# One long kernel of eight layers: other written orders of the pieces on five engines, and other places of the idle matmuls

## The reference, cut to what matters

```
x = x + L0_attn_a(ln(x))   # a recurrent state of 8x8 per head, one step per token (16 heads)
x = x + L0_ffn(ln(x))      # 8 experts, the best 2 by softmax, and a shared one (swiglu)
x = x + L0_attn_b(ln(x))   # best 15 of all earlier tokens, gathered; small MLP; a sampled palette
x = x + L0_ffn(ln(x))
x = x + L1_attn_a(ln(x))   # linear attention, running sums
x = x + L1_ffn(ln(x))      # 8 experts in bf16, the best 2 by sigmoid, and a shared one (relu squared)
x = x + L1_attn_b(ln(x))   # decaying state per head
x = x + L1_ffn(ln(x))
```

```
delta  = clip(v_t - k_t.S, -1, 1);  S = S + clip(0.9 * k_t delta, -1, 1);  o = clip(S.q_t, -1, 1)
```

## Time and profile before

| | us |
|---|---|
| timed runs: lowest, median, highest of 3 | 1463.68, 1468.32, 1477.88 |
| the profiled execution, first to last instruction | 1461.1 |
| PE busy, of which fill matmuls (585) | 1240.4, of which 178.1 |
| DVE busy | 1039.1 |
| POOL busy | 974.7 |
| ACT busy | 790.6 |
| first and last step of the scan on DVE | 44.3, 1196.8 |

### The profile page before, as it was taken

The page is one execution under the profiler, slowest core; times in us unless marked ns, Lnnn a source line. Parts: engine busy times, 40 slices in busy tenths (PEclk is TensorE's granted clock), DMA queues, the critical chain, the costliest instruction groups (busy, mean ns, idle before and its releaser), DMA issues.

```text
span 1461.1 us, 47169 instructions
## 1 busy us (share of the span) xinstructions
PE 1240.4 (85%) x18481; PEld 807.8 (55%) x18481; DVE 1039.1 (71%) x4444; ACT 790.6 (54%) x2119; POOL 974.7 (67%) x1398
## 2 busy tenths in 40 slices
PE   3787787888898988888899989988998989898886
PEld 1333444555556565655656565655656565656654
DVE  2778877888777877787687777978788775463532
ACT  1232243556466565658465556657474647566754
POOL 2553767786967677786776687877757567765541
PEclk9777687989999999999889999999899989999999
DMA  6000101001000000000000000100001010101000
GB/s 172 1 2 5 29 12 29 22 17 28 9 19 19 16 18 10 26 12 21 12 26 11 12 22 10 28 8 22 14 4 33 8 35 11 31 15 30 4 2 7
DMA packets 27208, 29.54 MB, mean 20 GB/s; under 512 B 12097, under 2 KB 22114, under 8 KB 26978
## 3 DMA queue, kind: packets, MB, share of 16 engines
q0 software_dynamic: 8304, 16.73, 4.4%
q1 hardware_dynamic: 18674, 9.71, 2.4%
HBM read 25.10 MB, written 2.29 MB: 19 GB/s over the span
## 4 chain that ended last, share of the span: by engine, by line
PE 36%; POOL 24%; DVE 20%; issue 9%; ACT 8%; SPq 1%; DMA 1%; POOLq 0%; DVEq 0%; ACTq 0%
POOL sb L1784 5%; POOL sb L1649 4%; DVE ps L964 4%; POOL sb L1646 3%; PE ps L665 3%; PE ps L717 3%; DVE ps L956 2%; PE ps L523 2%; PE ps L563 2%; PE ps L778 2%; PE ps L577 2%; POOL sb L1850 2%; PE ps L587 1%; PE ps L864 1%; PE ps L604 1%
## 5 line engine op out<-in xcount | busy, mean ns | idle before, releaser
L964 DVE TENSOR_TENSOR_SCAN ps<-ps,sb 128x47 f32<-128x47 f32 (+3 forms) x1024 | 271.0, 265 | 45.6 <-ACT sb L1373 1.5
L1784 POOL DMA_INDIRECT sb<-table,sb x240 | 244.7, 1020 | 86.7 <-issue 48.9
L956 DVE TENSOR_TENSOR ps<-sb,ps 128x24 f32<-128x24 f32 (+3 forms) x1024 | 193.2, 189 | 15.9
L523 PE MATMUL ps<-sb 128*128 128x512 bf16 x585 | 178.1, 415 | 7.7 <-ACT sb L1581 3.1
L1646 POOL TENSOR_TENSOR sb<-sb 128x1 f32<-128x1 f32 x128 | 74.4, 581 | 136.2 <-DVE sb L899 135.3
L1649 POOL TENSOR_SCALAR sb<-sb 128x128 f32<-128x128 f32 x128 | 103.8, 811 | 22.8 <-POOL sb L1646 22.0
L1297 ACT ACTIVATE sb<-ps 128x128 f32<-128x128 f32 x128 | 35.2, 277 | 136.4 <-PE ps L535 135.5
L577 PE MATMUL ps<-sb 32*32 32x32 f32 x2032 | 70.2, 209 | 43.6 <-DVE sb L936 42.6
L577 PEld LDWEIGHTS ps<-sb 32*32 32x32 f32 x2032 | 41.4, 108 | 114.0 <-DVE sb L936 72.2
L587 PEld LDWEIGHTS ps<-sb 32*32 32x32 f32 x2032 | 42.1, 108 | 100.2 <-issue 50.0
L587 PE MATMUL ps<-sb 32*32 32x12 f32 x2032 | 64.9, 189 | 28.9 <-DVE sb L972 21.5
(11 more groups left out here) (307 smaller groups left out, 3541.1 us busy)
## 6 DMA issues: line engine op xcount, KB each, us to landing
sb<-table,sb POOLq DMA_INDIRECT x240
sb<-in_cs SPq DMA_DIRECT2D x16, 128.0 KB
table<-sb SPq DMA_DIRECT2D x17, 64.0 KB, 1.5
sb<-in_x SPq DMA_DIRECT2D x4, 256.0 KB, 8.6
sb<-dscr SPq DMA_DIRECT2D x64, 2.0 KB
out<-sb SPq DMA_DIRECT2D x16, 64.0 KB
sb<-in_mdn POOLq DMA_DIRECT2D x1, 512.0 KB, 10.3
sb<-in_wex SPq DMA_DIRECT2D x1, 512.0 KB, 6.8
```

The source lines that it names most:

```text
L523: e.matmul(b[:, 0:512], identb[:, :], mup[:, 0:512], start=True, stop=True)
L956: e.tensor_tensor(at(psP, p + ROW - 3 - 2 * m, [ROW, 3], [2, m], [1, 2]), AC[:, row(n, k), :, HIST - 2 * m:HIST].rearrange("p r (a b) -> p ...
L964: e.tensor_tensor_scan(at(psD, 16 + k + COMB * skip, [COMB, 3 * ROW - skip]), at(psP, p + skip, [1, 3 * ROW - skip]), Q[:, i % 32, skip:3 ...
L1784: e.indirect_dma_start(GA[:, k, :], None, table[0:128 * i + 128, :] if i else table0, bass.IndirectOffsetOnAxis(u[:, k:k + 1], 0)).then_in ...
```

## The change

The strings of `ORDER` for all five engines and the digits of `FILL` are others. No instruction's form, tile or wait is changed. Each engine keeps the same number of pieces of each letter, so every real instruction of before is there again. Most pieces stand a few places earlier or later than before. On VectorE the letters of the scan shift by at most 7 places in 3856. The number of ScalarE's table loads stays at 60.

`FILL` now sums to 652 in place of 585. By the 20 rows of 112 digits: the first row has 79 in place of 98; the next fourteen (pieces 112 to 1679, which run from 139 to 1076 us in the trace of before) have 380 in place of 256; the last five have 193 in place of 231. Of these matmuls, 140 in place of 101 stand at pieces of the scan (letter s).

The diff replaces 104 lines of letters and digits; here are the first of TensorE's order, all of SyncE's, and the first and tenth of FILL:

```diff
@@ -107,116 +107,116 @@
 ORDER = {
     "PE":
...
-        "sfffsggffssggssfssgsfsssssgsssfssssssgsssssgsfsssgosoosossssffgssoossosasasasgsssaassasasasasgsssppfsssspsso"
...
+        "ffsfggffsgssgssfssgfsgssfsssssssssssssgsssgsfssssgosoosossossffssgossosasssaasgssaasassasasassgspspfssssssps"
...
     "SP":
-        "ppppmpppmpppmppmpppmppppmppppmppmppppmpmpppppmpmpppmppepemeppppmpeepemeeeeeeeeee",
+        "pppmpppmpppmpppmppppmepepppmeppmppemppppmepppempppepmepmppepmppeppmpppepmpmeeeee",
 }
 FILL = (
-    "0919090620400000025030020200100001010000101000001000500001020200007000090100000102000000000000002020000200020000"
...
-    "0001200000000000300000000010000000000000000010000000000000000040000000000000000000000000000000000000000020000000"
...
+    "3109100100002010005500000000000300000000200140003000600000002000030050060000000001002000000003000120000400000003"
...
+    "0001010000000000020000400000000002000200000000100000000100000000200003000000100000020010000000000003000000000000"
...
```

More of the change, by code:

```diff
@@ L115 @@
[L115 to L124, removed]
@@ new lines @@
+    "ACT":
+        "ffffffffffgffgsfffgfsfffffggffffsgsffggfffssffgooofooooffsfgffoaaaaaagsgppffpsffpfsppppogoooogooosaaaaaappps"
+        "ffffgsfmfmppmsmpgoppppfffffofooooomgmpmomfmmppsaafffaaammfpasgpgsmposoooooofffffmmmmpppgoppaagaaasmmpgfmmapp"
+        "mfmffpbbsfmbmbbbfppmlssollgooooollfffffommlgmmlppppopccsccccccccacccgcafmmfsaaadpmmaddddmffgfmmmfbgsbbbpogbf"
+        "fffpffopbppooooosmlllgmomlmllpmppaglppapaacapsgcccccsmcccccmpcccpmemefeeeseeeemmaeeeedddeddmmfffgbsbofmbbboo"
+        "ppobooommfmmfffpfplslolpppplllaagpplafaammgfmmacccccmcccmccccccmssmfeffeeepeeeeeedeebeeddfddmbbobbppgboooolo"
+        "offfffllsgsmlollmmpmpplgpapcapcfcccacaacccgccmcppcmmcameeeseeeedmmeeeedfdeeddmmefffbfmgbbbbssoppffpbfffooooo"
+        "ommmmpsflgpplolppppllaaflgaaaglmmmmfcffccacccccmccccmsccmmspfeegeeeeemeeedpeeebddddbbbesoffpfffbobpooooogmmm"
+        "lmllppplspolppppglamaaammmlafgmfacmffccfcccccccccccsmmepeeeeesedeeeeeeeddbbdfdsbbbgppmgoboooooommpmmlppsllop"
+        "pplllaafffpafaaflmmmccccccmccgcccmmgsccacmmeeeeedeeeeeeeeedsppdddbppmbbbbffobgomooooofffmmpsmllpplofppplllga"
+        "aaaapflffsffmmsmmcggcccccacccccmmcccpmmeeeeefeeeedeeeeeddddfspbbbbbmpbopoooooomfgffllmlmmspppofpllllpppffaff"
+        "fgccfsccccccccmmccccgmmaasaeeeeadgeeeepeeemmeeeddmdsdamgmofbbbbbooooboppffoffpmsmmmlsllopgppfffpfflllpmmlgpa"
+        "mamcccccccmmcccccsaaccmppamggeeeddeddeeemedefseeeeaegmbsopbbbboooopmmbpoomploppsllpppmmlllammlaaaappccccccmm"
+        "ccccccccmmeeeadeeeeeedesdeeeemddpbbbmbbmmmpobpoooppoolllpomppmlollpppalammaacmccacccccccccccmaedeemmeedeeddd"
+        "pbeeeeeebebbmbppbmmmmpppppbppbbblbllbpmmmllllmmmlllcccccccccclcclcclmmddddedeeleeeeeeeeeeepmmmmcbccmbbbbcccc"
+        "ccbcccccmmlmmllmmdeddddleemeeellmeeeeeeeelmccccccccbcccbbbccbcbeeeeeedeeeededllleeddlllelccccccccccccccdddee"
+        "eddeeeeeeeeeeeeeeeeeeeeeeeee",
@@ new lines @@
+    "POOL":
+        "ffffggfggggfffggggffggffgggggggoofooooooofgggagpffppppgpggoooogohoooohgagfhhhhghhhhhhhhhfpfppppfpooggggooooo"
+        "oofhhamfmhhggmhhhhhhhpgghhhhgfpofopppooooooopaggggfhhhhhhgggmbmphhhmhhfhhpppfflhhoollllpoolloloooogpcafggghh"
+        "ghghdhhhhhddhmmhhdfdmbgghffohopgggghoooolooflolppllppllalgpggchhhhhhhhehhhdhggmhmdmdddbhfpoogffhooppppoooool"
+        "pgglllfllallghhhhhhchhhmmedhhmbpghggffddddhhoopfphpglooooloolollplgllgpacgghhhhfehdhhhhhgmmhddmdbdfpggghffoh"
+        "hhpopooopoplooogfpllllagglllhchghhhhgmmhmefdhhgghbgpffhhhhddddoophoooolpppollglgoopllgagllhfchhhghhhhfggmmem"
+        "dhhhhbphhddddphoopppofooloooopglllfllgallgcghhhhhghhmmfedmhhgghpbddddhhhghoppopphoolooooollpfllalllfgfggghch"
+        "ghhmmfedhhhghhhbmpdhhghdddoogppphohlopooolofollpllllffacggghgegdhhhhhmmhghhdmdddfhhgghboogphhhoooooflpppoopf"
+        "flplllglgllacggmmegmdhghhhhgghhdhdhhhddbhoophhhooppooooploppgllalllllcmmhemdhhhhhhhhhhhhddbddphhoopppplooopl"
+        "looloollllachhhmmedhhhhmbhhhhdddpdhhhhpppppbllllllllhhhlhchllllmmllldemhhhhhhhhdhhddcdbldelllmmllllmddcddbed"
+        "llllllllddddceddddde",
@@ L224, in program @@
+    "0000000230000030003100000020008000210102000000020000001000000000000000004000000000000001000001030000000110000000"
+    "0000000000000000000000000000000000121502080000100000000020100000100005000000200208203201000000043000000030060100")
 def program(nc, t):
```

162 lines of the change are left out of this document (72 added, 90 removed).

## The result

After takes **1534.26 us** (median of 4 runs, 1525.59 to 1537.72), before 1468.05 (4 runs): ratio 1.0439, 95% interval 1.0393 to 1.0485. So it is 66 us slower. It lies outside the predicted range of 1436 to 1488 us and on the other side of the forecast. Run again later beside before, it took 1525.1 us for 1466.1: ratio 1.0422 (1.0388 to 1.0456).

What follows compares the result with a forecast made beforehand. No engine alone bounds the kernel: PE holds 36% of the path, POOL 24%, DVE 20%. Terms -1.4 + 7.6 - 11.8 - 1.9 + 1.5 = -6.0 us gave 1462.3 us against 1468.32; 8-of-10 range 1436 to 1488 us.

Steps and rivals of the forecast that it cites:

- All other moves: Pieces moved a few places on the engines: a worse place costs one wait, some 0.8 us, with like gains; 0.
- fill in the middle, its cost: 124 more fill matmuls on PE between 139 and 1076 us, 40.4 us, of which 0.189 on the path: +7.6 us.
- rival 2: 39 more fill matmuls in front of the scan's pieces make VectorE's scan wait: +20.9 us, 1489 us, chance 0.18.
- fill in the middle, its gain: Between 139 and 1076 us, half of 150 us at low clock returns to full clock on PE: -11.8 us.
- Fill at the end: 38 fewer fill matmuls in the last five rows of digits: -1.9 us; other end, clock falls, about +2 us.
- Start: One fill matmul instead of nine ahead of the first gram product, which begins 1.4 us earlier: -1.4 us.
- Gathers in groups: POOL's 240 gathers in 96 groups for 165; 69 more back-to-back pairs cost 6.2 us of POOL: +1.5 us.
- the sign that the prediction set for the layernorms: POOL's layernorms making PE wait longer at line 535 would show a term that was set to 0.
- SyncE: Queue stops at tile 1's output, delaying tile 6's `cs` to about 534 us; readers keep some 7 us: 0 us.
- its test: VectorE's wait on lines 577 and 587: near 88 us speaks against rival 2, above 105 us for it.
- Rivals 1 and 3: The first: new digits close waits, clock holds, 1441.4 us, chance 0.28; the third: orders of equal worth, 1468 us, 0.12.

Runs made afterwards that it cites:

- fitted fill: Fill remade to fit the idle times measured without fill, less 0.1 us: 1510.4 us (1.0282) on after's orders, 1469.5 us (1.001) on before's.
- experiment 3: Before with one engine's string from after: GpSimd 1.1032, VectorE 1.0974, ScalarE 1.1112, SyncE 0.996; also both orders spliced at 560 us without fill: 1.0606, 1.0638.

## Why the prediction was wrong

By its own steps:

- **All other moves, 0: failed, and the largest.** It said that a piece in a worse place costs one wait of some 0.8 us, that there are gains of the same kind, and that all of it lies inside the other ends. The orders alone cost 34.5 us (no fill) to 40 us (fitted fill). The step went from "moved by a few places" to "little", and experiment 3 shows how wrong that is: a mean shift of 1.5 to 1.8 places on one engine is worth 10%. Its evidence was thin besides. The 0.4 places by which gram was said to move are GpSimd's average with sign, where moves either way cancel; without sign it is 3.1 places, up to 17. And the 7 places hold for the scan on VectorE; on ScalarE its pieces move by up to 31. Why so small moves cost so much is argued, not shown: one late piece can make the next engines late, on a path of 4690 pieces, where the prediction let each wait be paid once.
- **Fill, -6.1 in all (7.6 - 11.8 - 1.9): failed.** Measured, the change of fill costs 66 - 34.5 = 31 us, or 26 if the orders are put at the 40 of the fitted pair.
- **Of it, fill in the middle, its cost, +7.6: failed.** It took the share of the present fill on the path, 0.189, for the new one, as if the new digits stood in places as good. All fill on the path went from 33.6 to 87 us. The premise, that new places match the waits of the new orders, could not be read from the trace of before. Its other end was rival 2's 22.7 us; the fill on the path grew by 53. Against a fill that fits, after's is 21 to 23 us too dear.
- **Fill in the middle, its gain, -11.8: failed.** The clock in the stretch went from 0.92 to 0.90, or stayed at 0.92 by the second profile; the sign of being right was a clock above 0.94.
- **Fill at the end, -1.9:** the clock fell from 0.96 to 0.92 there (0.93 in the second profile); the last tile's scan end to the end of the span grew from 264 to 269 us. The other end of that step, +2, was the right sign.
- **Start, -1.4:** not settled. In the profile of after, line 563's product began at 41.48 us, not at 39.8 (41.17 before), since the pieces ahead of it, POOL's line 1671 and then 1683, came later too. In the second profile it began at 39.09, and the scan's first step at 43.79 us for before's 44.30. First after, then its second profile:

```profile
34.00 3.93 PE L523 MATMUL ps<-sb 128*128 128x512 bf16 x9
39.21 0.30 PE L552 MATMUL ps<-sb 128*128 128x128 f32 x1 [1.29 <-POOL sb L1671]
41.48 1.97 PE L563 MATMUL ps<-sb 128*128 128x480 f32 x2 [1.65 <-POOL sb L1683]
```

```profile
39.09 3.56 PE L563 MATMUL ps<-sb 128*128 128x480 f32 x4 [1.43 <-POOL sb L1683]
```

- **Gathers in groups, +1.5:** not settled. The gathers themselves cost the same (line 1784 busy 241.2 us for 244.7 of before), and the sign that the prediction set for the layernorms behind the groups came only weakly: TensorE waits 28.1 us for line 1649 at line 535 in after, 24.4 in before. But GpSimd's string could not be judged apart: alone it costs 157 us, for want of the others.
- **SyncE, 0: right.** Ratio 0.996 with that string alone, though the queue does stop at the output: in that kernel tile 6's `cs` goes out at 558.94, behind an output at 558.03 us. Its reader on POOL starts at 564.86 without having waited, so the cover of some 7 us held, with 6 left.

```profile
503.71 0.33 SPq L1937 DMA_DIRECT2D table<-sb  x1
558.03 0.34 SPq L1962 DMA_DIRECT2D out<-sb  x1
558.42 0.42 SPq L1943 DMA_DIRECT2D dscr<-sb  x1
558.94 0.38 SPq L1931 DMA_DIRECT2D sb<-in_cs  x1
564.86 0.72 POOL L1751 TENSOR_TENSOR sb<-sb 128x256 f32<-128x256 f32 x1
```

**Rival 2** (fill in front of the scan, 1489 us) had the right side and the right sign of its test: the waits went past 105 us, to 138.8. It was still not the mechanism. Leaving out all 140 products at the scan's pieces changed nothing (1.0419 for 1.0422), and without any fill the wait for line 577 is 37 us longer in after's orders. The test that the prediction set for it did not tell it from a worse order; only the run with those products left out did. Rivals 1 and 3 fell with the clock and with the orders.

What stays open: which of the moves make after's orders 35 to 40 us worse. The loss is spread, 4 to 5 us a tile from tile 6 on; no single string of VectorE, ScalarE or GpSimd can be exchanged without paying more than the loss. That these strings fit as a set is shown; where after's fit each other less well is not. No run beat before clearly: the fitted fill on its orders is equal to it, and SyncE's string of after is at 0.996.

## What to carry to other kernels

Where the instructions of several engines stand in a written order and wait for each other every few microseconds, moves of a few places are not small until they are timed: price a new order at a few per cent, not at 0, and don't exchange one engine's order alone without timing it. Average moves without their sign, and look at the largest. A spare product that keeps TensorE busy belongs exactly ahead of a piece for which a wait was measured, and no longer than that wait; all of them one piece later were here worse than none. To place such products, take the idle times of a run without them.

## What the runs showed of the hardware

- **Time at half clock cost much less than half of itself.** From no fill to before's fill the mean clock went from 0.820 (span 1514.4 us) to 0.920 (1461.1 us): (0.18 x 1514.4 - 0.08 x 1461.1) / 0.5 = 311 us fewer at 1.2 GHz. 52 us were gained, or some 86 if the 33.6 us that the fill itself holds of the path are added. By the Trainium skill (TensorE: Matmul & The Clock Gate, Terms) the penalty is estimated as the throttled time times the lost share of the clock, half of the 311, 156 us; the runs show between a third and a little over half of that. TensorE holds 43% of the path without fill and 36% with it, and the prediction's way, that share of the 156 us, gives 56 to 67 us before the fill's own cost, which is nearer.
- **The same program differs by 3.5% between chips.** Before took 1465 to 1469 us on three chips of the experiments and 1517.5 and 1519.5 on two. On the latter the mean granted clock is lower in before's runs (0.890 to 0.904, for 0.907 to 0.923 on the others), and the chain of every profile names "another core or an unknown queue" with up to 3%, which no profile of the others does. `B_spA`, equal to before but for SyncE, has waits there of up to 9.0 us that nothing recorded ends:

```profile
ACT sb L1593 <- remote: 12.9, 3, 9.0
DVE sb L972 <- remote: 10.1, 3, 5.4
```

  What these waits are, and whether they or the clock come first, was not tried. VectorE's, ScalarE's and GpSimd's instructions last the same there (line 964: 265 ns on both).
